# GpSimd's sum of tokens and attention's result in eight pieces, one behind each scatter of sorted rows

## The chip, the cores and the metric

One core of one Trainium2 chip runs the whole program. The metric is the device time of one execution in microseconds; the kernel before took 1020.18 us in the median of 3 runs (1018.56 to 1020.27). TensorE does the matrix products (PE in the rows), VectorE (DVE), ScalarE (ACT) and GpSimd (POOL) the rest, SyncE (SP) issues most transfers. GpSimd issues the scatters, whose addresses are computed in the kernel.

## The reference, cut to what matters

Two layers over x of 2 batches of 1024 tokens with 128 features. Each layer is attention and then a feed-forward part, with a layer norm behind every part. What the change touches is the second half of layer 0:

```
x = x + mla_attention(rmsnorm(x, norm1_w), ...)          # "attention's result" is added to the tokens
x = x + moe(rmsnorm(x, norm2_w), gate_w, gate_b, W1, b1, W2, b2)
x = layernorm(x)

def moe(x, ...):
    logits = x @ gate_w.T + gate_b
    top = argmax(logits)                                   # one of 4 experts for each token
    h = relu(W1[top] x + b1[top]);  return W2[top] h + b2[top]
```

Layer 0 begins with a retention layer of 8 heads and a layer norm; the latent attention has 16 heads of 8 features; layer 1 is an attention with 16 heads and a product with ternary weights.

## The kernel before, in words

All activations stay on the chip: X holds the tokens as 16 tiles of 128 tokens x 128 features (8 tiles for each of the 2 batches), U holds, while the experts work, the result of the latent attention.

The first stage (retention) loops over the 16 tiles. Everything after it is one stage with an order written out by hand: `order()` makes a list of events, (kind, number), and each engine runs through the same list and does its share of every event. So each engine takes its instructions in a fixed order, and waits for the others by semaphores. The base of the list are units of attention: "S" (scores of a unit, TensorE, then exponentials on ScalarE), "A" (scores once more for their maxima, TensorE, then a reduction on VectorE, 12 units ahead), "V" (product with the values). When the maxima of a block are there, "M" turns them and "split" on GpSimd divides them into three bfloat16 parts and writes them with three transfers to the stacks of queries (lines 1331 to 1341). Between the units lie the events of the experts, placed by `experts_of(b)` for batch b (lines 1044 to 1057):

- "square" and "norm": mean square of the tokens, and hn = normalised tokens, with the number of each token behind its features
- "H", "G", "C": logits, the expert of each token, and the row (slot_i) that each token has when tokens are sorted by expert; VectorE writes slot_i at line 1987
- "sort" (lines 1353 to 1359, GpSimd): eight indirect DMAs, one for each tile of 128 tokens, scatter the rows of hn to `sorted_rows` in HBM. Each adds 16 to the semaphore e_sorted
- "steer" and "bias" (VectorE): tables of which expert a tile of sorted rows belongs to
- "base" (lines 1360 to 1366, GpSimd): U = X + U for the batch's eight tiles in one instruction of 128x1024. The helper link() lets GpSimd wait for the instruction's own end. In batch 0 a small product of a bias follows
- `route(b)` on SyncE's queue: load_steer, then load_sorted (line 1211), which waits for e_sorted to be 16 x 8 and loads the sorted rows in three transfers of 4, 4 and 3 tiles, then the weights of each tile's expert (line 1232)
- "x": TensorE transposes the sorted rows (line 1652) as soon as their load has landed; then "h", "y" for 11 tiles (lines 1667 and 1675), "put" (line 1371, GpSimd), which scatters each tile of results back to the order of the tokens, fetch_rows on SyncE, and "sum" (line 1378), which adds U and the fetched rows to X

In the list the event "split" of block 12 comes behind "base" in batch 0; in batch 1 no event of GpSimd stands between "sort" and "base", and the next "split" comes well behind them.

Of the kernel before, what the change touches and what calls it, by code (L numbers as in the profile page):

```python
# [13 lines left out]
ALU = mybir.AluOpType  # L14
# [5 lines left out]
NT = T // P  # L20
# [171 lines left out]
def build(nc, d, out, phases=5):  # L192
    ctx = ExitStack()
    with ctx:
# [21 lines left out]
        X = A.tile(NTILE, P)  # L216
# [10 lines left out]
        U = A.tile(NTILE, P)  # L227
# [134 lines left out]
        def chain(eng, s):  # L362

            def link(ins):
                counts[s.name] = counts.get(s.name, 0) + 1
                ins.then_inc(s, 1)
                eng.wait_ge(s, counts[s.name])
            return link
# [788 lines left out]
        def attention():  # L1157
# [4 lines left out]
            def _(sp):  # L1162
# [57 lines left out]
                def load_steer(b):  # L1220
                    sp.wait_ge(e_steered, b + 1)
                    _, values = nc.values_load_multi_w_load_instructions(
                        whose_i[0:1, 0, :], (mybir.EngineType.SP,), min_val=0, max_val=(NE - 1) * HID,
                        skip_runtime_bounds_check_because="a count of at most 3 of 3 comparisons, times 512")
                    return values
# [76 lines left out]
            def _(pool):  # L1302
                g_ = nc.gpsimd
                link = chain(pool, pool_step)
                for kind, k in order():
# [9 lines left out]
                    elif kind == "ln3":  # L1315

                        t = slice(QT * k, QT * (k + 1))
# [24 lines left out]
                    elif kind == "norm":  # L1342

                        t = slice(k * NT, (k + 1) * NT)
# [8 lines left out]
                    elif kind == "sort":  # L1353

                        pool.wait_ge(e_placed, k + 1)
                        pool.wait_ge(xs_cleared, 16 * B)
                        for t in range(NT):
                            g_.indirect_dma_start(xs_dram[k], bass.IndirectOffsetOnAxis(slot_i[:, t:t + 1], 0),
                                                  hn[:, t, :], None).then_inc(e_sorted[k], 16)
                    elif kind == "base":  # L1360

                        t = slice(k * NT, (k + 1) * NT)
                        link(g_.tensor_tensor(U[:, t, :], X[:, t, :], U[:, t, :], ALU.add))
                        if k == 0:
                            pool.wait_ge(load4, 48)
                            g_.tensor_scalar(bqs, bqk[:, 0:1], QSCALE, None, ALU.mult).then_inc(bias_scaled, 1)
                    elif kind == "put":

                        b, i = k
# [3 lines left out]
                    elif kind == "sum":  # L1373

                        for c in range(2):
                            t = slice(k * NT + QT * c, k * NT + QT * (c + 1))
# [3 lines left out]
                    elif kind == "root":  # L1380

                        t = slice(k * NT, (k + 1) * NT)
# [7 lines left out]
                    elif kind in ("L", "R") and k < 3:  # L1390

                        t = slice(k * QT, (k + 1) * QT)
# [28 lines left out]
            def _(pe):  # L1421
# [9 lines left out]
                for kind, k in order():  # L1431
# [222 lines left out]
                    elif kind == "h":  # L1654

                        b, i = k
                        if i == 0:
                            pe.wait_ge(e_steered, b + 1)
                            _, steer[b] = nc.values_load_multi_w_load_instructions(
                                whose_i[0:1, 0, :], (mybir.EngineType.PE,), min_val=0, max_val=(NE - 1) * HID,  # L1660
                                skip_runtime_bounds_check_because=why)
# [219 lines left out]
            def _(dve):  # L1881
# [19 lines left out]
                for kind, k in order():  # L1901
# [116 lines left out]
                    elif kind == "y":  # L2018

                        b, i = k  # L2020
                        if i == 0:
                            dve.wait_ge(e_steered, b + 1)
                            _, steer[b] = nc.values_load_multi_w_load_instructions(
                                whose_i[0:1, 1, :], (mybir.EngineType.DVE,), min_val=0, max_val=(NE - 1) * P,
                                skip_runtime_bounds_check_because="a count of at most 3 of 3 comparisons, times 128")
# [123 lines left out]
```

## Time and profile before

| what | value |
|---|---|
| median of 3 runs | 1020.18 us (1018.56 to 1020.27) |
| the profiled execution, its own time | 1024.54 us |
| its span (first to last instruction) | 1022.1 us |
| busy: TensorE, VectorE, ScalarE, GpSimd | 890.6, 762.3, 655.0, 392.0 us |
| sum of "base", line 1363 | 2 instructions, 4.0 us |
| scatters of "sort", line 1358 | 16 instructions, 15.7 us |
| chain that ended last, share of the span | TensorE 50%, VectorE 27%, ScalarE 7%, DMA 4%, GpSimd 3% |

Busy time is the time in which an engine executes something; the chain is followed back from the last instruction, at each step to what released it. The experts of batch 0 lie at 444 to 535 us of the span, those of batch 1 at 632 to 740 us. Times in the rows are microseconds from the start of the span.

### The profile page before, as it was taken

The numbers are of one execution on the slowest core, as the hardware profiler recorded it, in microseconds if no ns is written. First come the engines' busy times: TensorE is split into PE (matmuls) and PEld (weight loads), VectorE is DVE, ScalarE is ACT, GpSimd is POOL, SyncE is SP. The second block draws the span as 40 slices with busy tenths as digits, with TensorE's granted clock in tenths as the row PEclk, the third lists the DMA queues.
The fourth block names the chain that finished last, engine by engine and source line by source line (L and its number), as shares of the span: only waits on it lengthen the run. The fifth ranks groups of instructions, "written<-read, shape, count | busy, mean of one in ns | idle before, by whom it ended". The sixth has DMA issues, their size and how long they took to land.

```text
span 1022.1 us, 22793 instructions
## 1 busy us (share of the span) xinstructions
PE 890.6 (87%) x9065; PEld 445.1 (44%) x9070; DVE 762.3 (75%) x1155; ACT 655.0 (64%) x1285; POOL 392.0 (38%) x607
## 2 busy tenths in 40 slices
PE   5999999998877889988798778879988999999983
PEld 3778677777632343333472322216422222222232
DVE  3667766856487678886458498776889999999954
ACT  2554655655526678774446547765767988898981
POOL 2755757878332552134345111352432111111240
PEclk8999999999899999997799899989999999999997
DMA  8000000200501034111420601032206100000000
GB/s 294 1 1 2 1 1 2 73 2 1 150 1 41 21 128 138 38 43 52 122 74 2 199 21 38 5 92 85 75 2 187 32 20 20 21 20 2 5 23 21
DMA packets 49405, 52.51 MB, mean 51 GB/s; under 512 B 8874, under 2 KB 40618, under 8 KB 49140
## 3 DMA queue, kind: packets, MB, share of 16 engines
q1 hardware_dynamic: 45012, 48.12, 15.5%
q0 software_dynamic: 4288, 2.94, 1.1%
q8 instruction: 72, 1.18, 0.5%
q14 instruction: 33, 0.27, 0.1%
HBM read 32.37 MB, written 19.68 MB: 51 GB/s over the span
## 4 chain that ended last, share of the span: by engine, by line
PE 50%; DVE 27%; ACT 7%; issue 6%; DMA 4%; POOL 3%; SPq 2%; another core or an unknown queue 1%; DVEq 0%; ACTq 0%; POOLq 0%
DVE arena L1930 19%; PE banks L1592 10%; PE banks L1557 7%; PE banks L1477 5%; ACT arena L1750 3%; PE banks L740 3%; PE banks L485 3%; PE banks L495 2%; PE banks L1667 2%; PE banks L1675 2%; PE banks L673 2%; DMA arena<-arena 1%; PE banks L735 1%; PE banks L699 1%; ACT arena L521 1%
## 5 line engine op out<-in xcount | busy, mean ns | idle before, releaser
L1930 DVE TENSOR_REDUCE arena<-banks 128x2 f32<-128x1024 f32 (+1 forms) x384 | 440.9, 1198 | 65.4 <-PE banks L1477 33.0
L1750 ACT ACTIVATE arena<-banks 128x512 f32<-128x512 f32 (+1 forms) x768 | 409.4, 587 | 120.9 <-PE banks L1557 77.7
L1592 PE MATMUL banks<-arena 128*9 128x256 f32 (+1 forms) x3328 | 257.0, 385 | 6.8 <-ACT arena L1763 4.6
L1557 PE MATMUL banks<-arena 61*128 61x512 bf16 (+4 forms) x896 | 167.5, 373 | 33.9 <-ACT arena L1750 23.7
L1477 PE MATMUL banks<-arena 56*128 56x512 bf16 (+3 forms) x896 | 165.2, 371 | 29.1 <-DVE arena L1930 22.1
L1557 PEld LDWEIGHTS banks<-arena 61*128 61x128 bf16 (+1 forms) x896 | 44.7, 93 | 194.5 <-ACT arena L1750 160.8
L1331 POOL CAST arena<-arena 16x128 bf16<-16x128 f32 x32 | 9.0, 282 | 301.0 <-ACT arena L1818 292.3
L1592 PEld LDWEIGHTS banks<-arena 128*9 128x9 f32 x3328 | 51.6, 89 | 133.0 <-issue 86.7
L1477 PEld LDWEIGHTS banks<-arena 56*128 56x128 bf16 x896 | 45.2, 95 | 54.6 <-DVE arena L1930 40.9
L383 POOL TENSOR_TENSOR arena<-arena 128x8 f32<-128x8 f32 (+1 forms) x35 | 51.3, 1466 | 30.2 <-DVE arena L2094 27.8
L1341 POOL DMA_DIRECT2D arena<-arena x96 | 55.2, 579 | 10.7 <-POOL arena L1334 9.2
L521 ACT ACTIVATE arena<-banks,arena 128x128 f32<-128x128 f32 x128 | 46.4, 477 | 0.5 <-PE banks L504 0.5
L1371 POOL DMA_INDIRECT expert_rows<-arena x22 | 21.4, 972 | 54.9 <-DVE arena L2026 54.9
L1927 DVE TENSOR_REDUCE arena<-banks 128x4 f32<-128x1024 f32 (+1 forms) x32 | 30.4, 954 | 16.2 <-PE banks L1487 13.5
L511 ACT ACTIVATE arena<-banks 128x1024 f32<-128x1024 f32 x16 | 16.4, 1022 | 39.9 <-PE banks L740 39.9
L554 DVE TENSOR_TENSOR arena<-banks,arena 128x128 f32<-128x128 f32 x16 | 4.7, 291 | 47.0 <-PE banks L495 47.0
L1746 ACT ACTIVATE arena<-banks 128x512 f32<-128x512 f32 (+1 forms) x64 | 27.9, 490 | 17.2 <-PE banks L1566 16.9
L529 ACT ACTIVATE arena<-banks 128x1024 f32<-128x1024 f32 x16 | 16.4, 1026 | 33.9 <-PE banks L485 32.5
L767 DVE TENSOR_TENSOR arena<-banks,arena 128x1024 f32<-128x1024 f32 x16 | 19.6, 1223 | 24.0 <-PE banks L673 23.9
L485 PE MATMUL banks<-arena 128*128 128x128 f32 x256 | 33.9, 287 | 2.6 <-DVE arena L770 2.6
L673 PE MATMUL banks<-arena 128*128 128x512 f32 x64 | 32.8, 637 | 1.7 <-DMA arena<-c_gk 1.7
L866 POOL TENSOR_TENSOR arena<-arena 128x512 f32<-128x512 f32 x16 | 25.3, 1578 | 22.5 <-DVE arena L770 22.5
(239 smaller groups left out, 1463.5 us busy)
## 6 DMA issues: line engine op xcount, KB each, us to landing
arena<-k_products SPq DMA_DIRECT2D x32, 224.0 KB
arena<-q_products SPq DMA_DIRECT2D x64, 112.0 KB
q_products<-arena SPq DMA_DIRECT2D x16, 384.0 KB, 3.3
k_products<-arena SPq DMA_DIRECT2D x16, 384.0 KB, 3.8
arena<-e_w SPq DMA_DIRECT2D x22, 256.0 KB
arena<-arena POOLq DMA_DIRECT2D x96, 4.0 KB, 1.7
sorted_rows<-c_pads SPq DMA_DIRECT2D x2, 709.5 KB, 8.6
arena<-sorted_rows SPq DMA_DIRECT2D x4, 258.0 KB, 3.1
```

Of the source, the lines that this page charges most:

```text
L383: link(eng.tensor_tensor(y, v, epst[:, 1:2].to_broadcast(list(v.shape)), ALU.pow))
L485: ins = nc.tensor.matmul(bank(s // 4)[:, (s % 4) * P:(s % 4 + 1) * P], wg[:, s * P:(s + 1) * P], XT[:, i, :], start=True, stop=True)
L521: ins = nc.scalar.activation(ga[:, s, :], bank(4 + s // 4)[:, (s % 4) * P:(s % 4 + 1) * P], ACT.Identity, scale=gn[:, 0, s:s + 1], bias=gn ...
L673: ins = nc.tensor.matmul(bank(c), XT[:, n + 1, :], wqk[:, c * 512:(c + 1) * 512], start=True, stop=True)
L740: ins = nc.tensor.matmul(bank(2 + s // 4)[:, (s % 4) * P:(s % 4 + 1) * P], sm[:, s, :], vv[n % 2][:, s, :], start=first, stop=True, skip_g ...
L1341: g_.dma_start(rows, nmp[k % 2][:, i, :]).then_inc(mrow[k % 2], 16)
L1477: ins = nc.tensor.matmul(bank(first + par)[:, at:at + hi - lo], Qs[k_][rows, qc, y, qo:qo + P], Ks[k_][rows, y, lo:hi], start=True, stop=n ...
L1557: ins = nc.tensor.matmul(bank(S_BANK + (use + par) % SCORES)[:, at:at + C - o], Ks[n % NS][rows, y, kt * P:(kt + 1) * P], Qs[n % NS][rows, ...
L1592: ins = nc.tensor.matmul(PS[h * VROWS:h * VROWS + VW, AV_BANK, o:end], V[:, b, kt, HG * g + h, :], Pr[u % PROBS][:, h, o:end], start=(kt = ...
L1750: s_.activation(Pr[s % PROBS][:, 2 * x + par, o:C], scores[:, o:C], ACT.Exp) \
L1927: v_.tensor_reduce(of, two_banks.rearrange("p r (y e) -> p r y e", y=2)[:, :, :, 0:width], AX.X, ALU.max).then_inc(ring_dve, 1)
L1930: v_.tensor_reduce(of[:, :, x], two_banks[:, :, 0:width], AX.X, ALU.max).then_inc(ring_dve, 1)
```

## The change

The event "base" no longer does the sum. Each tile's sum now stands directly behind the scatter of that tile in the event "sort", as an instruction of 128x128, and each is linked: GpSimd waits for its end before it takes the next scatter. The bias product of batch 0 stays in "base". What is computed is the same.

```diff
@@ -1355,12 +1355,12 @@
                         pool.wait_ge(e_placed, k + 1)
                         pool.wait_ge(xs_cleared, 16 * B)
                         for t in range(NT):
+                            i = k * NT + t
                             g_.indirect_dma_start(xs_dram[k], bass.IndirectOffsetOnAxis(slot_i[:, t:t + 1], 0),
                                                   hn[:, t, :], None).then_inc(e_sorted[k], 16)
+                            link(g_.tensor_tensor(U[:, i, :], X[:, i, :], U[:, i, :], ALU.add))
                     elif kind == "base":
 
-                        t = slice(k * NT, (k + 1) * NT)
-                        link(g_.tensor_tensor(U[:, t, :], X[:, t, :], U[:, t, :], ALU.add))
                         if k == 0:
                             pool.wait_ge(load4, 48)
                             g_.tensor_scalar(bqs, bqk[:, 0:1], QSCALE, None, ALU.mult).then_inc(bias_scaled, 1)
```

## Rows read from the trace of the kernel before

**Rows 1.** The page: its span, and busy us (share of span) xinstructions.
```profile
span 1022.1 us, 22793 instructions
PE 890.6 (87%) x9065; PEld 445.1 (44%) x9070; DVE 762.3 (75%) x1155; ACT 655.0 (64%) x1285; POOL 392.0 (38%) x607
```
**Rows 2.** Timeline, GpSimd, batch 0: start, duration, engine, line, operation, [idle before <-releaser].
```profile
475.95 1.09 POOL L1358 DMA_INDIRECT sorted_rows<-arena  x1 [7.41 <-DVE arena L1987]
477.35 0.99 POOL L1358 DMA_INDIRECT sorted_rows<-arena  x1 [0.30 <-issue]
...
485.00 0.96 POOL L1358 DMA_INDIRECT sorted_rows<-arena  x1 [0.30 <-issue]
485.99 2.01 POOL L1363 TENSOR_TENSOR arena<-arena 128x1024 f32<-128x1024 f32 x1
...
488.31 0.28 POOL L1331 CAST arena<-arena 16x128 bf16<-16x128 f32 x1
```
**Rows 3.** Timeline, SyncE's queue, batch 0.
```profile
487.29 1.48 SPq L1218 DMA_DIRECT2D arena<-sorted_rows  x3
488.97 25.66 SPq L1232 DMA_DIRECT2D arena<-e_w  x11
```
**Rows 4.** Timeline, TensorE, batch 0.
```profile
488.46 1.04 PE L1592 MATMUL banks<-arena 128*9 128x256 f32 x8
490.29 1.96 PE L1652 MATMUL banks<-arena 128*128 128x128 f32 x8 [0.79 <-DMA arena<-sorted_rows]
```
**Rows 5.** Chain that ended last, batch 0: start, duration, what.
```profile
478.73 8.56 issue
487.29 2.87 DMA arena<-sorted_rows
```
**Rows 6.** Groups by line, GpSimd: shapes, count | busy us, mean ns | idle before, releaser.
```profile
L1332 POOL TENSOR_TENSOR arena<-arena 16x128 f32<-16x128 f32 x32 | 12.9, 402 | 2.7
L571 POOL TENSOR_TENSOR arena<-arena 128x512 f32<-128x512 f32 x6 | 6.5, 1091 | 0.3
L866 POOL TENSOR_TENSOR arena<-arena 128x512 f32<-128x512 f32 x16 | 25.3, 1578 | 22.5 <-DVE arena L770 22.5
L1351 POOL TENSOR_TENSOR arena<-arena 128x1024 f32<-128x1024 f32 x2 | 3.8, 1898 | 0.2
```
**Rows 7.** Timeline, GpSimd, first put of batch 0.
```profile
503.96 1.07 POOL L1371 DMA_INDIRECT expert_rows<-arena  x1 [11.91 <-DVE arena L2026]
```
**Rows 8.** Timeline, GpSimd, batch 1.
```profile
664.92 1.09 POOL L1358 DMA_INDIRECT sorted_rows<-arena  x1 [7.29 <-DVE arena L1987]
...
673.94 0.96 POOL L1358 DMA_INDIRECT sorted_rows<-arena  x1 [0.30 <-issue]
674.93 2.01 POOL L1363 TENSOR_TENSOR arena<-arena 128x1024 f32<-128x1024 f32 x1
685.64 0.28 POOL L1331 CAST arena<-arena 16x128 bf16<-16x128 f32 x1 [8.71 <-issue]
```
**Rows 9.** Timeline, SyncE's queue, batch 1.
```profile
676.32 1.48 SPq L1218 DMA_DIRECT2D arena<-sorted_rows  x3
681.65 31.71 SPq L1232 DMA_DIRECT2D arena<-e_w  x11
```
**Rows 10.** Timeline, TensorE, batch 1, during the scatters.
```profile
670.33 0.62 PE L1592 MATMUL banks<-arena 128*9 128x256 f32 x8
```
**Rows 11.** Transfers issued from 660 to 700 us: KB each, median us to landing.
```profile
arena<-sorted_rows SPq DMA_DIRECT2D x2, 258.0 KB, 3.3
```
**Rows 12.** Timeline, TensorE, batch 1, transposition of sorted rows.
```profile
688.15 0.66 PE L1652 MATMUL banks<-arena 128*128 128x128 f32 x4
```
**Rows 13.** Timeline, ScalarE, batch 0, behind the scatters.
```profile
486.84 2.38 ACT L1750 ACTIVATE arena<-banks 128x512 f32<-128x512 f32 x4 [3.59 <-remote]
```
**Rows 14.** Chain that ended last, batch 1, during the scatters.
```profile
670.07 3.49 another core or an unknown queue
674.67 1.88 another core or an unknown queue
```

## The prediction

> **What bounds the kernel now.** I read the page first, then the timeline of the one engine that the change edits, GpSimd, then the rows of those who wait for it, and last the chain of work that ended last in the same stretch. The page [rows 1] shows TensorE at 87% and GpSimd at 38% of a span of 1022.1 us, so GpSimd is not short of time: 607 instructions and 392 us of work. What it does can only matter where somebody waits for a result of it. The sum X+U of line 1363 is a result that nobody waits for: one instruction of 2.01 us in each batch [rows 2, 8], and nobody needs U before the event "sum", when the experts' rows have been fetched back. The scatters of line 1358 are the opposite.
>
> The rows of GpSimd for batch 0 [rows 2] show eight scatters. The first starts at 475.95 as soon as VectorE has placed the rows (7.41 us idle before it, ended by line 1987). The second starts at 477.35, 0.30 us after the end of the first; the eighth starts at 485.00 and ends at 485.96. So a step of the burst is 0.96 + 0.30 = 1.26 to 1.27 us, and the burst takes 10.01 us. The sum starts 0.03 us behind the last scatter (485.99), and then comes the splitting of the next maxima (488.31).
>
> SyncE waits for all eight scatters together (line 1212: e_sorted at 16 x 8) and issues the loads of the sorted rows at 487.29 [rows 3], 2.29 us after the eighth scatter began (487.29 - 485.00). TensorE has ended its last product before that at 488.46 + 1.04 = 489.50, and its transposition of the sorted rows starts at 490.29 behind 0.79 us of idle time which the load ended [rows 4]. The chain says the same [rows 5]: it goes through a stretch of 8.56 us called "issue", which is SyncE waiting while GpSimd scatters, and then through 2.87 us of the load. So in batch 0 the end of the last scatter sets when TensorE goes on, and TensorE takes its instructions in a fixed order: everything behind the transposition, of all engines, is put off with it. That is the row that decides this case.
>
> **The change, part by part.** Removed: per batch one sum of 128x1024 behind the eight scatters. Added: per batch eight sums of 128x128, one behind each scatter, each with a link(), that is a wait of GpSimd for its own sum before it goes on. Behind that wait stand the next scatter and, behind the last one, the splitting of maxima. Nothing else moves: no DMA is added, and steering, loads and puts keep their places.
>
> The price of a sum of 128x128. The trace has 128x512 at 1.091 us (line 571) and 128x1024 at 1.898 and 2.008 us (lines 1351 and 1363) [rows 2, 6]; from 1.091 to 2.008 is 0.917 us for 512 columns, 0.00179 a column, so 128 columns cost 1.091 - 384 x 0.00179 = 0.40 us. The sum of 16x128 of line 1332, with the same number of columns on fewer partitions, takes 0.402. I take 0.40. Between the end of a scatter and the start of a sum lie 0.03 us [rows 2].
>
> The price of what the sum does to the scatter behind it. There is a gap of 0.30 us ahead of a scatter, whether a scatter stands before it [rows 2] or not; I take it unchanged, with the link's wait inside it. A scatter that follows another kind of instruction took 1.09 us (475.95) and 1.09 us (664.92), and the first put behind other work 1.07 us (503.96), against 0.96 to 0.99 us for one that follows a scatter [rows 2, 7, 8]. In the changed kernel each of the eight follows another kind of instruction. I take 1.07 us; the bounds are 0.97 and 1.09.
>
> So a step becomes 0.03 + 0.40 + 0.30 + 1.07 = 1.80 us instead of 1.27. From the start of the first scatter to the end of the eighth it is 1.09 + 7 x 1.80 = 13.7 us instead of 10.0: **the eighth scatter ends 3.7 us later**. Lower bound: scatters stay at 0.97, step 1.70, 1.09 + 11.9 = 13.0, 3.0 us later. Upper bound: a sum that follows a scatter pays for the change of kind as well, as 2.008 against 1.898 us of the same sum behind other work suggests (0.11 us): step 1.91 to 1.93, 4.5 us later.
>
> Batch 0: the cover of the scatters is gone already (TensorE idles 0.79 us there), so all of it lands on the path: loads issued at 487.29 + 3.7 = 491.0, transposition at 494.0 instead of 490.29. **+3.7 us.** The 2.29 us from the last scatter to the load stay: batch 1 has 676.32 - 673.94 = 2.38 us with the same code [rows 8, 9], and I see nothing in them that a wider spacing shortens. What is late behind it is late by the same amount, because it all hangs from the transposition: the experts' weights are issued behind the sorted loads on the same queue (488.97) [rows 3], and puts, fetch and sum of tokens follow the experts. TensorE's clock: it was already at half speed here (a product group of line 1592 takes 1.04 us at 488.46, against 0.62 us at full clock) [rows 4, 10]. A longer idle stretch might hold it there a little longer; I put zero on it and keep 1.7 us as its upper bound (a further stretch of 3.7 us in which products take 1.04 for 0.62 would lose 3.7 x 0.42/1.04 = 1.5, rounded up).
>
> Splitting of the maxima in batch 0: GpSimd is free after 13.7 + 0.03 + 0.40 = 14.1 us instead of 10.0 + 0.03 + 2.01 = 12.1, that is 2.1 us later. Its three transfers feed scores of block 12, while block 11 has only begun and all of the experts' work stands in between. Zero. Without that cover it would cost up to those 2.1 us.
>
> Batch 1: the eighth scatter ends at 674.90 + 3.7 = 678.6, the loads are issued at 680.0 instead of 676.32 and take 1.48 us to issue, till 681.5. The next thing on SyncE's queue is the first expert weight, which went out at 681.65 [rows 9]: 0.1 us of room, and at the upper bound it goes out 0.7 us late, in front of products at 691.7. The sorted rows land some 3.3 us after issue [rows 11], so at about 683.5 to 685; TensorE transposes at 688.15 [rows 12]. Hidden, and GpSimd itself is idle until 685.64 [rows 8]. **+0.** If the 8.5 us of room were gone it would cost another 3.7.
>
> The removed 2.01 us return nothing: they lie behind the scatters, where nobody waits.
>
> Sum: 0 x 2.01 + 3.7 + 0 = +3.7 us. The profiled execution took 1024.54 us with a span of 1022.1, so 2.4 us lie around the span, and it stands 4.4 us above the median of 1020.18. I expect a span near 1025.8 in a profile, and for the median 1020.18 + 3.7 = **1023.9 us** (+0.36%).
>
> One rule speaks to the price of the sum. In the rows, a sum of 128x512 takes 1.091 us at line 571 and 1.578 us at line 866, a factor 1.45 [rows 6]; the second runs in the first stage, while VectorE is multiplying and adding tiles. The Trainium skill, "GPSIMD Engine Reference", Specifications, says that GpSimd shares its SBUF interfaces with VectorE and contends with VectorE's instructions that have two SBUF inputs. By that rule the small sums, which now run while VectorE makes the steering tables, would be stretched, and the one big sum of before, at 486 us, was not. The trace agrees only in part: VectorE's work beside the burst is mostly reduction out of PSUM.
>
> **The rivals.**
> (a) The sums are stretched by VectorE. Each takes 0.40 x 1.45 = 0.58 us, 7 x 0.18 = 1.3 us more: +5.0 us, 1025.2. For it: 1.578 against 1.091. Against: the scatters themselves kept 0.96 to 0.99 all along, and VectorE's two-input work there is a dozen instructions of 0.2 us.
> (b) Faster: the burst itself disturbs the others, and spreading it mends that. In both bursts ScalarE and VectorE stood still although TensorE's products had been done: ScalarE 3.59 us before 486.84 with an unnamed releaser [rows 13], and in batch 1 the chain has 3.49 and 1.88 us of "unknown queue" [rows 14]. In batch 0 that lies ahead of the wait for the load and is covered by it; in batch 1 it is on the chain. If a step of 1.80 us instead of 1.27 lets it vanish, batch 1 gains 5.4 us and about 2.1 us more, since TensorE's half clock after it vanishes with it (three rounds of scores, maxima and products; where a group of products takes 1.04 for 0.62 us [rows 4, 10], a round loses some 0.7): 3.7 - 5.4 - 2.1 = -3.8 us, 1016.4. It decides from the point where the gain in batch 1 exceeds 3.7 us. Against: it may belong to the profiled execution alone, which is 4.4 us longer than the median, or it goes on for as long as scatters are in flight, and then the longer burst adds some: +1.9 us more, 1025.8.
> (c) No change to measure: half of that disturbance goes (the 3.49 us), 3.7 - 3.5 = +0.2 us, 1020.4; or, with the same outcome, the wait at the transposition has cover in an undisturbed run that I can't see.
> (d) That the change doesn't do what it says: the link's wait might let the next scatter start while the sum runs. The rows speak against it: behind every linked instruction the next one starts only after its end.
>
> **How the numbers follow.** Forecast of +3.7 with its bounds 3.0 to 4.5: 0.62. (a) 0.07. The longer disturbance of (b), 1025.8: 0.05. (b) itself 0.10. (c) 0.14. (d) 0.02: the scatters are then put off by nothing, 1020. A measurement of this kernel can tell about 0.2%, 2.0 us, from no change: slower is all from 1022.2 up, so 0.62 + 0.07 + 0.05 = 0.74; the same 0.14 + 0.02 = 0.16; faster 0.10. The range leaves out (b) and the far end of the late cases: 1020.0 to 1026.0, which takes in (c), the bounds of the forecast, (a), and most of the 1.7 us of the clock.
>
> **What would show it.** In the changed profile: eight sums of 128x128 at 0.39 to 0.58 us between the scatters; scatters 1.70 to 1.93 us apart; SyncE's loads of the sorted rows about 3.7 us later against the first scatter (15.0 instead of 11.3 us behind it) in both batches; TensorE's idle time at line 1652 in batch 0 grown from 0.79 to some 4.5 us, and none in batch 1. It would be wrong if TensorE's wait in batch 0 didn't grow by that, if the unnamed waits of ScalarE vanished or doubled, or if the scatters stayed 1.27 us apart.

## The result, and the profile after

The changed kernel takes 1023.68 us in the median (1022.27 to 1028.81, 8 runs), the kernel before beside it 1020.2 us (1018.56 to 1022.02, 8 runs). The ratio is 1.0049, with a 95% interval of 1.0031 to 1.0067: slower by some 5.0 us (0.0049 x 1020.2) by the ratio, by 3.5 us by the two medians. The profiled executions stand the other way: 1022.82 us with a span of 1020.8 after, 1024.54 us and 1022.1 before [rows 1]. This contradiction is taken up behind the experiments.

The page of the changed kernel, as in rows 1 its span, and busy us (share of span) xinstructions:

```profile
span 1020.8 us, 22812 instructions
PE 886.5 (87%) x9070; PEld 442.6 (43%) x9070; DVE 763.8 (75%) x1155; ACT 654.7 (64%) x1285; POOL 393.8 (39%) x621
```

GpSimd's timeline in batch 0 of the changed kernel, to be read against rows 2 (start, duration, engine, line, operation, [idle before <-releaser]):

```profile
474.18 1.09 POOL L1359 DMA_INDIRECT sorted_rows<-arena  x1 [7.37 <-DVE arena L1987]
475.29 0.43 POOL L1361 TENSOR_TENSOR arena<-arena 128x128 f32<-128x128 f32 x1
476.00 1.00 POOL L1359 DMA_INDIRECT sorted_rows<-arena  x1 [0.28 <-POOL arena L1361]
477.03 0.41 POOL L1361 TENSOR_TENSOR arena<-arena 128x128 f32<-128x128 f32 x1
...
486.22 0.97 POOL L1359 DMA_INDIRECT sorted_rows<-arena  x1 [0.28 <-POOL arena L1361]
487.23 0.42 POOL L1361 TENSOR_TENSOR arena<-arena 128x128 f32<-128x128 f32 x1
...
487.96 0.28 POOL L1331 CAST arena<-arena 16x128 bf16<-16x128 f32 x1
```

The idle time ahead of a scatter is now ended by line 1361, the sum: the link holds the next scatter back. A step is 0.97 + 0.03 + 0.42 + 0.28 = 1.70 us (the first three are 1.82, 1.73 and 1.72) where it was 1.27, and the burst, from the start of the first scatter to the end of the eighth, takes 487.19 - 474.18 = 13.01 us for 10.01.

SyncE's queue in the same kernel, batch 0 and batch 1 (rows 3 and 9 answer to them):

```profile
488.53 1.89 SPq L1218 DMA_DIRECT2D arena<-sorted_rows  x3
490.63 26.15 SPq L1232 DMA_DIRECT2D arena<-e_w  x11
...
681.34 2.92 SPq L1218 DMA_DIRECT2D arena<-sorted_rows  x3
684.53 27.65 SPq L1232 DMA_DIRECT2D arena<-e_w  x11
```

TensorE's timeline, batch 0, and last its transposition in batch 1 (rows 4 and 12):

```profile
484.97 0.62 PE L1592 MATMUL banks<-arena 128*9 128x256 f32 x8
491.45 1.09 PE L1652 MATMUL banks<-arena 128*128 128x128 f32 x4 [5.86 <-DMA arena<-sorted_rows]
493.46 1.09 PE L1652 MATMUL banks<-arena 128*128 128x128 f32 x4 [0.92 <-DMA arena<-sorted_rows]
495.44 1.04 PE L1592 MATMUL banks<-arena 128*9 128x256 f32 x8
...
686.96 0.66 PE L1652 MATMUL banks<-arena 128*128 128x128 f32 x4
```

The wait for the sorted rows in batch 0 was 0.79 us [rows 4] and is 5.86 + 0.92 us. In batch 1 there is none: the loads go out 681.34 - 666.97 = 14.37 us behind the first scatter, before 11.40 [rows 8, 9], and TensorE still comes later than they land.

The chain that ended last, batch 0 of the changed kernel (start, duration, what), runs through the burst and the load, as it did in rows 5:

```profile
474.18 1.09 POOL sorted_rows L1359
475.29 0.44 POOL arena L1361
475.73 0.27 issue
476.00 1.00 POOL sorted_rows L1359
...
486.22 2.29 DMA sorted_rows<-arena
...
488.96 4.36 DMA arena<-sorted_rows
```

Each sum of 128x128 and each 0.27 us behind it is now a piece of the chain. What the profile of after doesn't have is the unnamed waits of rows 13 and 14: during the scatters of batch 1 the chain goes through VectorE and TensorE with no "unknown queue" at all.

The spans are made of stretches that can be compared one by one. From the start of the last put to the end all kernels need 293 to 295 us. The start of the first scatter (474 to 479 us) and the stretch from the last put of batch 0 to the first scatter of batch 1 (135 to 139 us) differ by some microseconds from one execution to the next, the first of them with the same code ahead of it. What an experiment moves is mostly the two stretches from a batch's first scatter to its first put. These are what the table below gives, "scatter to put" for short, from the rows of lines 1358 and 1371 of each profiled execution.

### The profile page after: what moved, and what is told of

It is laid out like the page before. It is cut to its first block, busy times and chain, and to the rows that moved or that the text cites. A ratio compares the mean times of both kernels' runs of the same rounds, so it can differ in the third digit from the quotient of the medians.

```text
span 1020.8 us, 22812 instructions
## 1 busy us (share of the span) xinstructions
PE 886.5 (87%) x9070; PEld 442.6 (43%) x9070; DVE 763.8 (75%) x1155; ACT 654.7 (64%) x1285; POOL 393.8 (39%) x621
## 4 chain that ended last, share of the span: by engine, by line
PE 49%; DVE 28%; ACT 6%; issue 6%; DMA 4%; POOL 4%; SPq 2%; DVEq 0%; ACTq 0%; POOLq 0%
DVE arena L1930 20%; PE banks L1592 10%; PE banks L1557 7%; PE banks L1477 5%; ACT arena L1750 3%; PE banks L740 3%; PE banks L485 3%; PE banks L495 2%; PE banks L1667 2%; PE banks L1675 2%; PE banks L673 2%; DMA arena<-arena 1%; PE banks L735 1%; ACT arena L521 1%; PE banks L699 1%
## 5 line engine op out<-in xcount | busy, mean ns | idle before, releaser
L1927 DVE TENSOR_REDUCE arena<-banks 128x4 f32<-128x1024 f32 (+1 forms) x32 | 30.4, 954 | 14.6 <-PE banks L1487 13.5
```

Of the source, the lines that this page charges most:

```text
L1927: v_.tensor_reduce(of, two_banks.rearrange("p r (y e) -> p r y e", y=2)[:, :, :, 0:width], AX.X, ALU.max).then_inc(ring_dve, 1)
```

## The experiments

Differences are against the kernel before, which ran beside every group of experiments: 1024.37 us in the median beside the first four (1019.43 to 1027.84), 1021.73 beside the next four and 1023.55 beside the last four, which ran on another chip (pieces in one batch "the same again", the change later by one more, and the pause alone). That its own median moves by 4 us between groups, while within a group it serves as the measure, will matter.

| kernel | scatter to put, batch 0 | batch 1 | median us | ratio, 95% |
|---|---|---|---|---|
| before | 28.01 | 31.71 | 1020.2 | |
| the change | 32.02 | 28.50 | 1023.68 | 1.0049 (1.0031 to 1.0067) |
| pieces in batch 0 alone | 31.07 | 31.61 | 1027.56 | 1.0026 (1.0007 to 1.0045) |
| the same again | 30.84 | 31.92 | 1027.37 | 1.0034 (1.0012 to 1.0056) |
| pieces in batch 1 alone | 27.48 | 28.45 | 1020.19 | 0.9967 (0.9949 to 0.9985) |
| the same again | 26.47 | 28.46 | 1020.38 | 0.9962 (0.9941 to 0.9984) |
| eight pieces behind the scatters | 26.65 | 32.40 | 1022.78 | 0.9990 (0.9973 to 1.0007) |
| a second instruction per piece | 35.65 | 31.45 | 1033.07 | 1.0080 (1.0058 to 1.0101) |
| the change again | 29.86 | 27.53 | 1027.43 | 1.0059 (1.0039 to 1.0079) |
| four pieces, batch 1 alone | 27.98 | 29.03 | 1021.95 | 1.0006 (0.9995 to 1.0017) |
| before, experts later | 25.88 | 26.93 | 1016.31 | 0.9945 (0.9926 to 0.9964) |
| the change, experts later | 29.41 | 27.77 | 1020.49 | 0.9992 (0.9976 to 1.0008) |
| the change, later by one more | 28.34 | 27.73 | 1018.52 | 0.9947 (0.9924 to 0.9970) |
| a pause alone, batch 1 | 26.79 | 27.66 | 1019.5 | 0.9957 (0.9935 to 0.9978) |

**One batch at a time.** The sum stays in one piece in the other batch.

```diff
                         for t in range(NT):
+                            i = k * NT + t
...
+                            if k == 0:
+                                link(g_.tensor_tensor(U[:, i, :], X[:, i, :], U[:, i, :], ALU.add))
...
                     elif kind == "base":
-                        t = slice(k * NT, (k + 1) * NT)
-                        link(g_.tensor_tensor(U[:, t, :], X[:, t, :], U[:, t, :], ALU.add))
+                        if k == 1:
+                            t = slice(k * NT, (k + 1) * NT)
+                            link(g_.tensor_tensor(U[:, t, :], X[:, t, :], U[:, t, :], ALU.add))
```

> The eight pieces stand behind the scatters in batch 0 only; batch 1 keeps the one sum of 128x1024. My theory (the whole cost is TensorE's wait for the sorted rows of batch 0): as slow as the full change, +3.0 to +4.0 us, ratio 1.0035 (1.003 to 1.005). Rival (both batches pay, or GpSimd's longer occupation costs by itself): about half of the change, +1.8 us, ratio 1.0018. The eighth scatter of batch 0 should end 13.0 us behind the start of the first, as in the changed kernel, that of batch 1 10.0 us.

With `k == 1` and `k == 0` exchanged:

> The eight pieces stand behind the scatters in batch 1 only; batch 0 keeps the one sum of 128x1024. My theory: batch 1 has 8.5 us of room between the landing of the first sorted rows and their transposition, so no change, within 1 us, ratio 1.000 (0.999 to 1.001). Rival (both batches pay): +1.8 us, ratio 1.0018. Rival of the late signals (the dense burst delays TensorE's signals, and wider spacing mends that in batch 1, where it lies on the chain): up to -5 us, ratio 0.995 to 0.998, and no unnamed wait of ScalarE in batch 1 of the profile, while batch 0 may show one.

Pieces in batch 0 alone cost 0.26%, 2.7 us, and in batch 1 alone they gain 0.33%, 3.4 us. Both were run a second time beside the last group:

> Pieces in batch 0 only, once more. The burst lasts 13.0 instead of 10.0 us, and from its start to the first put it takes 31 us instead of 27.5: +3.5 us, ratio 1.0035 (1.0025 to 1.0045). Rival (parts don't add up, batch 0 bears all of the change's 5 to 6 us): 1.005 or more.

> Pieces in batch 1 only, once more. Two effects are known from traces by now: late signals of TensorE behind a dense burst (31.6 to 32.4 us from the first scatter to the first put of batch 1 where they are, 26.9 where they are not; 27.5 to 28.5 with pieces), and VectorE's tables stretched by the pieces (+0.9 us in batch 1). If the late signals belong to the ordinary runs too: faster again, ratio 0.996 to 0.998. If the first 0.9967 was chance and only the stretched tables are left: ratio 1.000 to 1.002.

The answers were +0.34% (3.5 us) and -0.38% (3.9 us). So the two halves of one change have opposite signs. The batch that loses is the one in which TensorE waits for the sorted rows. The batch that gains is one in which the forecast had seen nothing at all in the sum, and something in its rival (b). Here is ScalarE in batch 1 where the burst is dense (pieces in batch 0 alone, the second time), and VectorE beside it:

```profile
674.17 1.29 ACT L1754 ACTIVATE arena<-banks 128x512 f32<-128x512 f32 x2 [3.50 <-remote]
...
675.59 1.23 DVE L1934 TENSOR_REDUCE arena<-banks 128x2 f32<-128x1024 f32 x1 [2.55 <-remote]
```

and its chain through the same stretch:

```profile
670.66 3.48 another core or an unknown queue
...
675.46 1.67 another core or an unknown queue
```

"Remote" and "unknown queue" mean that the profile finds no releaser. Both engines wait for TensorE's products here, and these had been done for some microseconds (the last section has the rows of one such wait side by side), so by these rows it is TensorE's signal that comes late. The signal itself is in no row, and that both engines waited for something else is not excluded. These are rows 13 and 14 again, in another kernel. Over all 14 profiled executions the picture is: such waits in 9 of the 12 bursts with scatters 1.27 us apart, and in none of the 16 bursts that have something between the scatters. In the rows of batch 1 they are worth 3.8 us: scatter to put takes 31.91 in the mean of the four kernels that have them there (31.71, 31.61, 31.92, 32.40), and 28.07 in the six with eight pieces (28.50, 28.45, 28.46, 27.53, 27.77, 27.73).

**Is it the pieces or their place?** The eight linked sums are kept, but all of them stand behind the eighth scatter.

```diff
                         for t in range(NT):
...
+                        for i in range(k * NT, (k + 1) * NT):
+                            link(g_.tensor_tensor(U[:, i, :], X[:, i, :], U[:, i, :], ALU.add))
                     elif kind == "base":
-                        t = slice(k * NT, (k + 1) * NT)
-                        link(g_.tensor_tensor(U[:, t, :], X[:, t, :], U[:, t, :], ALU.add))
```

> The sum is done in eight linked pieces as in the change, but all of them behind the eighth scatter. My theory (not the pieces cost, but that they stand between the scatters): no change, within 1 us, ratio 1.000 (0.999 to 1.001), though GpSimd works 8 x 0.49 = 3.9 us there instead of 2.0 and the splitting of maxima in batch 0 starts 1.9 us later. Rival (the splitting of maxima or the longer work of GpSimd is what costs): +1.5 to +2 us, ratio 1.0015 to 1.002.

No difference (0.9990, the interval takes in 1), although GpSimd works longer at it:

```profile
486.00 3.87 POOL L1361 TENSOR_TENSOR arena<-arena 128x128 f32<-128x128 f32 x8
```

3.87 us for 2.01, and the splitting of the maxima 1.9 us later, cost nothing. So neither the number of instructions nor GpSimd's time is the price; only what stands ahead of the eighth scatter counts. It also keeps the late signals in both batches, which the pieces between scatters remove.

**Is the dose right?** Each piece gets a second linked instruction, a multiplication of the same 128x128 by 1.

```diff
                             link(g_.tensor_tensor(U[:, i, :], X[:, i, :], U[:, i, :], ALU.add))
+                            link(g_.tensor_scalar(U[:, i, :], U[:, i, :], 1.0, None, ALU.mult))
```

> The change with a second linked instruction of 128x128 behind each piece, a multiplication of U by 1.0 (about 0.3 to 0.4 us with its gap). My theory (every microsecond between the scatters of batch 0 goes 1:1 to the end): 7 x 0.35 = 2.5 us more than the change, about +6.1 us against the kernel before, ratio 1.006 (1.005 to 1.007); still nothing from batch 1. Rival (the delay saturates, or some other wait takes it over): no more than +4.5 us, ratio 1.0045.

GpSimd and TensorE in batch 0 of this kernel:

```profile
481.81 1.06 POOL L1359 DMA_INDIRECT sorted_rows<-arena  x1 [0.28 <-POOL arena L1362]
482.89 0.43 POOL L1361 TENSOR_TENSOR arena<-arena 128x128 f32<-128x128 f32 x1
483.41 0.53 POOL L1362 TENSOR_SCALAR arena<-arena 128x128 f32<-128x128 f32 x1
...
501.59 1.94 PE L1653 MATMUL banks<-arena 128*128 128x128 f32 x8 [10.89 <-DMA arena<-sorted_rows]
```

The burst takes 17.76 us instead of 13.0, and scatter to put in batch 0 35.65 instead of 30.95 (the mean of the four kernels with pieces there and the experts' place unchanged: 32.02, 31.07, 30.84, 29.86): 4.7 us of burst, 4.7 us of path. Batch 1 has run out of room too (31.45 for 28.07). Against the kernel before that is 35.65 - 27.23 = +8.4 in batch 0 and 31.45 - 31.91 = -0.5 in batch 1, +7.9 in all; timed, it is 0.80% of 1024.37, 8.2 us. The forecast of 6.1 us was too low because its dose was: the second instruction lengthens a step by 0.67 us, not by 0.35. In batch 1 TensorE now waits for the sorted rows too, 3.26 us.

**The change once more**, beside the second group:

> The changed kernel itself once more, on the same chip as the next three. With batch 0 alone at 1.0026 and batch 1 alone at 0.9967, three readings are possible. If the parts add up (batch 0 pays about 3.7 us, batch 1 gains about 3.4): 0 to +1 us, ratio 1.000 (0.998 to 1.002). If the first measurement of the change holds: +3.5 to +5 us, ratio 1.0035 to 1.005. In the profile, no unnamed wait of ScalarE or VectorE in either batch.

1.0059: the loss is confirmed, here at 6.0 us (0.0059 x 1021.73), above the range of the second reading, and the parts do not add up to it. The 14 executions of the changed kernel fall into two groups with nothing between them: seven take 1022.3 to 1024.2 us (five of the first eight, two of these six) and seven 1026.7 to 1028.8. Their mean granted clock is 0.959 and 0.956. That the median is 1023.68 the first time and 1027.43 the second is a matter of how many fell into which. Both profiled executions, 1022.82 and 1022.43 us, are of the lower group, so no trace shows what the upper one has.

**How little is enough to keep the gain of batch 1?** Batch 0 stays as before; in batch 1 a sum of two tiles stands behind every second scatter.

```diff
+                            if k == 1 and t % 2:
+                                link(g_.tensor_tensor(U[:, i - 1:i + 1, :], X[:, i - 1:i + 1, :], U[:, i - 1:i + 1, :], ALU.add))
```

> Batch 0 as in the kernel before; in batch 1 the sum is done in four pieces of 128x256, one behind every second scatter, so scatters come in pairs and the mean step is 1.27 + 0.5 x 0.7 = about 1.6 us. If the density of the whole burst delays TensorE's signals (eight scatters in 10 us), the late signals of batch 1 shrink or vanish and the kernel is about 3 us faster than before, ratio 0.997, like the pieces behind every scatter of batch 1. If each scatter has to have its own pause, half or more of the late signals stay (2 to 5 us of unnamed waits in batch 1), ratio 0.998 to 1.000.

The profile shows the burst at 11.99 us, no late signals, and 29.03 us to the put. The time is that of the kernel before (1.0006, up to 1.0017). That is neither of the two expected outcomes: the late signals are gone from the profile and the time is no better. Two things may lie behind it. Beside this group the kernel before had 1021.73 us, so there may have been little to gain. And the longer sums (128x256, 0.65 us) hold up VectorE's tables more: the last of them starts 7.34 us behind the first scatter, against 6.23 in the kernel before and 6.79 in the changed one. The run doesn't settle how wide a pause must be.

**Is it cover that batch 0 lacks?** In the hand-written order the experts of batch 0 (its sorted rows and all behind) are put off by two units of attention, so that TensorE has work while GpSimd scatters. First in the kernel before, then in the changed one, then in the changed one with three units.

```diff
-            pace, tile, end = ((4, 12, 17), (2, 15, 24))[b]
+            pace, tile, end = ((4, 14, 19), (2, 15, 24))[b]
```

> The kernel before with the experts of batch 0 two units of attention later in the order (transposition of the sorted rows, products, puts and sum of tokens), sum in one piece. The wait for the sorted rows gets some 4.5 us more of cover. TensorE's wait at the transposition goes from 0.8 us to 0. If the late signals behind the dense burst are a delay of their own, they are now uncovered and the gain is at most 1 to 2 us, ratio 0.998 to 1.000; the unnamed waits of batch 0 stay. If they cost nothing, 3 us faster, ratio 0.997.

> The changed kernel with the same shift by two units in batch 0. TensorE waits 5.9 + 0.9 us for the sorted rows in the change; two units cover 4.5 us. My theory (the change's loss in batch 0 is this wait and nothing else): 4 to 5 us faster than the change itself, TensorE's wait at the transposition down to 1 to 2.5 us, and faster than the kernel before, ratio 0.996 to 0.999. Rival (the pieces cost time elsewhere in batch 0): no faster than the change by over 1 us.

With (4, 15, 20) in the changed kernel:

> The changed kernel with the experts of batch 0 three units of attention later. Two units left TensorE 2.0 + 0.5 us of waiting for the sorted rows. My theory (in batch 0 the loss is that wait alone): with three units the wait is gone and the kernel is some 1.5 to 2.5 us faster than with two, ratio to before 0.995 to 0.998, and it comes within 1 to 2 us of the kernel before with two units (0.9945). Rival (the pieces cost something else of 3 us or more, that no cover takes away): no faster than with two units, 0.999 or more.

TensorE at the transposition of batch 0 in the three kernels, in this order:

```profile
492.42 0.66 PE L1652 MATMUL banks<-arena 128*128 128x128 f32 x4
493.96 0.63 PE L1652 MATMUL banks<-arena 128*128 128x128 f32 x4 [0.88 <-DMA arena<-sorted_rows]
```
```profile
491.62 0.63 PE L1652 MATMUL banks<-arena 128*128 128x128 f32 x4 [2.04 <-DMA arena<-sorted_rows]
492.75 0.63 PE L1652 MATMUL banks<-arena 128*128 128x128 f32 x4 [0.50 <-DMA arena<-sorted_rows]
```
```profile
495.33 0.66 PE L1652 MATMUL banks<-arena 128*128 128x128 f32 x4
496.29 0.63 PE L1652 MATMUL banks<-arena 128*128 128x128 f32 x4 [0.30 <-DMA arena<-sorted_rows]
```

In the changed kernel the wait of 5.86 + 0.92 us shrinks to 2.04 + 0.50 with two units and to 0.30 with three, and its time against the kernel before goes from 1.0059 to 0.9992 and 0.9947. But the shift also helps the kernel before, by 5.6 us, more than the 3 us that were expected at most; it helps the changed one by 6.8 us, where 4 to 5 were expected. At the same place, two units later, the changed kernel is still 0.47% slower, 4.8 us (0.9992 against 0.9945): TensorE waits 2.54 against 0.88 us, and scatter to put is 3.5 us longer (29.41 for 25.88). Both still wait for their rows there, so the longer burst still shows. Whether the loss goes away when both are covered would need the kernel before with three units, which was not run. So these three runs show that TensorE's wait shrinks with cover and that the time falls by at least as much; they don't show that the pieces cost nothing beside it. That the loss hangs on what stands ahead of the eighth scatter of batch 0 rests on the pieces behind the scatters, on batch 0 alone and on the dose. The kernel before with two units, 1016.31 us (1012.95 to 1018.58) beside 1021.73, beats both kernels of this case.

**Is it the sum or the pause?** In the last experiment the sums stay in one piece in both batches, and in batch 1 GpSimd fills a tile of 192 columns that nobody uses (`spare`) behind each scatter.

```diff
+                            if k == 1:
+                                link(g_.memset(spare, 0.0))
```

> The kernel before, with a linked memset of 128x192 of an unused tile (about 0.4 us, no operand read) behind each scatter of batch 1; the sums stay in one piece. It gives batch 1 the pauses of the change without a GpSimd instruction that reads two operands. If sharing the way to SBUF is what stretches VectorE's tables there: line 2000 stays at 0.21 us where the change shows 0.41 to 0.50, line 1995 at 0.17 instead of 0.49. If the pause keeps TensorE's signals in time: no unnamed waits in batch 1. Time: like the pieces in batch 1 or up to 0.9 us faster, ratio 0.996 to 0.999 if late signals count in ordinary runs, 1.000 if not.

Its batch 1, and then ScalarE in its batch 0, where the burst is dense:

```profile
663.74 1.09 POOL L1360 DMA_INDIRECT sorted_rows<-arena  x1 [7.28 <-DVE arena L1991]
664.81 0.29 POOL L1363 MEMSET arena<- 128x192 f32 x1
665.39 1.01 POOL L1360 DMA_INDIRECT sorted_rows<-arena  x1 [0.29 <-POOL arena L1363]
...
486.21 1.09 ACT L1754 ACTIVATE arena<-banks 128x512 f32<-128x512 f32 x2 [4.28 <-remote]
```

0.9957, a gain of 4.4 us, with work that does nothing but take 0.27 to 0.29 us between scatters. The same execution has a late signal in batch 0 and none in batch 1. So what gains in batch 1 is the pause. Whether it is cheaper this way than by the sums can't be told: 27.66 us to the put is less than their mean of 28.07, but lies within their 27.53 to 28.50, and the intervals of the times overlap.

There is a difference on VectorE, though. Batch 1, the tables of the experts, first in the kernel before, then in the changed one, then with the pause alone (there four lines further down):

```profile
667.24 0.17 DVE L1995 TENSOR_SCALAR arena<-arena 128x12 int32<-128x12 f32 x1
...
670.42 0.21 DVE L2000 SCALAR_TENSOR_TENSOR arena<-arena 128x48 f32<-128x48 f32 x1
670.91 0.21 DVE L2000 SCALAR_TENSOR_TENSOR arena<-arena 128x48 f32<-128x48 f32 x1
```
```profile
669.28 0.49 DVE L1995 TENSOR_SCALAR arena<-arena 128x12 int32<-128x12 f32 x1
...
672.54 0.50 DVE L2000 SCALAR_TENSOR_TENSOR arena<-arena 128x48 f32<-128x48 f32 x1
...
673.32 0.41 DVE L2000 SCALAR_TENSOR_TENSOR arena<-arena 128x48 f32<-128x48 f32 x1
```
```profile
666.05 0.32 DVE L1999 TENSOR_SCALAR arena<-arena 128x12 int32<-128x12 f32 x1
...
669.23 0.21 DVE L2004 SCALAR_TENSOR_TENSOR arena<-arena 128x48 f32<-128x48 f32 x1
```

In the kernel with the sums three instructions grow by 0.32, 0.29 and 0.20 us. Part of the first is covered by the instruction behind it: the last of the tables starts 6.79 us behind the first scatter instead of 6.23, so all three together cost 0.56 us. In the kernel with the filling the first grows by 0.15, line 2004 (line 2000 before) not at all, and the last table starts at 6.22 us.

## Why the prediction was right, and where not

**The time.** Forecast was 1023.9 us and 1023.68 was measured. Part of that is luck: the second time the same kernel had 1027.43 us, the burst grew by less than was forecast, and batch 1, which was put at nothing, holds two terms that were left out. What follows takes the terms one by one.

**The step of the burst: right in kind, one term mis-sized.** Forecast 0.03 + 0.40 + 0.30 + 1.07 = 1.80 us, measured 0.03 + 0.42 + 0.28 + 0.97 = 1.70. The term that failed is the scatter behind another kind of instruction: behind a sum it takes 0.97 us, hardly more than behind another scatter. Only the first of the burst takes 1.09, in both kernels. The evidence in rows 2, 7 and 8 had been scatters behind 7 to 12 us of idle time, never one behind a short sum. The burst grew by 3.0 us, my lower bound, not by 3.7.

**"All of it lands on the path of batch 0: +3.7": the number came out, but not by its working.** Scatter to put is 27.23 us in the mean of the six kernels with the sum in one piece and the experts in their place (28.01, 27.48, 26.65, 27.98, 26.47, 26.79), and 30.95 in the four with pieces: +3.7. Of these 3.0 are the burst: the first transposition starts 14.3 to 14.6 us behind the first scatter in the six and 17.3 to 17.6 in the four. The other 0.7 lies between the first transposition and the put: 12.1 to 13.7 us in the six (mean 12.9), 12.5 to 14.8 in the four (mean 13.6). Two things differ there. In the changed kernel TensorE waits 0.92 us more for the second load, which takes 4.36 us in the chain against 2.87 [rows 5]. And TensorE's clock, whose part I had at zero: the two product groups behind the transposition take 1.04 us each, the half clock, where the stretch is 13.7 us (the kernel before, four pieces) and 0.62 us each, the full clock, where it is 12.1 and 12.2 (pieces in batch 1 the second time, the pause alone). It was at the half clock ahead of the wait as well in the changed kernel, in three groups of four (1.04 us from 479.15 on, 0.62 at 484.97), so the wait is not shown to be what lowers it. As the two ranges overlap, the 0.7 is not clear of noise. Alone in batch 0, timed, the pieces cost 2.7 and 3.5 us.

**"TensorE idles 0.79 us there" was read from a disturbed execution.** The wait grew by 5.07 us at its first part (5.86 - 0.79), more than the burst. In the profile of before TensorE itself had come 2.1 us late to this point, held up by ScalarE's wait for a late signal [rows 13], which hid most of the wait for the load. In the changed kernel TensorE ends its last group ahead of the wait at 484.97 + 0.62 = 485.59, 11.41 us behind the first scatter; in the kernel before the rows had come 490.29 - 475.95 = 14.34 us behind it [rows 2, 4]. So an undisturbed execution of before waits 14.34 - 11.41 = 2.9 us, and the change adds 5.86 - 2.9 = 3.0, the growth of the burst. The kernel with four pieces in batch 1 has the dense burst in batch 0 without late signals, and there the wait stands in a row:

```profile
492.20 1.97 PE L1656 MATMUL banks<-arena 128*128 128x128 f32 x8 [3.28 <-DMA arena<-sorted_rows]
```

So 3.3 us by this execution. The argument survived, since any hole at that point makes the burst critical; the size of the hole did not.

**Splitting of maxima and the room of batch 1: right; the issue of the loads was mis-sized.** The splitting of maxima stood 13.78 us behind the first scatter instead of 12.36, 1.4 us later for the forecast 2.1, and the experiment with the pieces behind the scatters put it off by 1.9 us at no cost. In batch 1 the loads took 2.92 us to issue instead of the 1.48 that I had kept, the first weight went out at 684.53, 0.27 us behind them, and TensorE waited for neither. The removed 2.01 us returned nothing, as forecast.

**"Batch 1: +0" failed.** Two terms were not in the forecast. The late signals, 3.8 us where they occur, go away with the pauses; that is the mechanism of rival (b), and experiment and rows bear it out: -3.4, -3.9, and -4.4 us with the pause alone. I had dismissed it as something that "may belong to the profiled execution alone". Against it stand the four pieces, with no late signal in the profile and no gain in time. And the sums stretch VectorE's tables by 0.56 us. The nearest to a bound for a burst without either is the kernel before with later experts, whose profile has no late signal in batch 1: 26.93 us to the put, against 28.07 with pieces. So batch 1 costs 1.1 us by this one execution where before is undisturbed, and gains 3.8 where it is not.

**Rival (a) fell, its cause turned round.** The small sums took 0.41 to 0.45 us beside VectorE, not 0.58; VectorE's instructions took 0.50 for 0.21. The Trainium skill, "SBUF — State Buffer", Who interferes with whom, states that a VectorE instruction with two SBUF inputs contends with a GpSimd instruction that reads SBUF, and not with one that only writes it. From kernel to kernel the trace agrees: line 2000 has two inputs and takes 0.50 and 0.41 us in the changed kernel and 0.21 in the one with the filling. Row by row it agrees in part. GpSimd at that time, in the changed kernel:

```profile
672.23 0.97 POOL L1359 DMA_INDIRECT sorted_rows<-arena  x1 [0.28 <-POOL arena L1361]
673.23 0.42 POOL L1361 TENSOR_TENSOR arena<-arena 128x128 f32<-128x128 f32 x1
```

VectorE's 0.41 us from 673.32 on lie beside a sum, but the 0.50 from 672.54 on lie beside a scatter, and so do the 0.49 of line 1995, which has one input; in the dense burst scatters leave both lines short. What lengthens those two is open.

**Rival (c)** (no measurable change) fell by the interval, and (d) by the releasers in GpSimd's rows.

**Why slower in time and faster in the profile.** The profiled execution of before has late signals in both batches and costs 1024.54 us, that of the change has none. Batch by batch the rows give 28.01 to 32.02 (+4.0) and 31.71 to 28.50 (-3.2), +0.8 together; the first burst of before began 1.8 us later (475.95 for 474.18), and with that noise the changed profile is the shorter one, by 1.3 us. If most ordinary runs of before had no late signals in batch 1, the change should cost 3.7 + 1.1 = 4.8 us; timed it was 5.0 and 6.0. If most had them, 3.7 - 3.8 = -0.1. The group of the first comparison had a median of before of 1020.2, that of the second 1021.73, while the single batches ran beside 1024.37 and 1023.55. This fits: the parts were measured beside a slower kernel before than the whole was, and so -3.4 and +2.7 need not add up to +5.0. It is argued, not shown, as the ordinary runs leave no rows and the change was not timed beside a before of 1024 us. A second reason is certain: the profiled execution of before, 1024.54 us, is longer than all its eight runs beside the change (1022.02 at most), while the two profiled executions of the change come from the lower of its two groups.

**What stays open.** How often late signals occur in runs without a profile, and what makes them. What makes half of the changed kernel's executions some 5 us longer than the rest. So the 5.0 and 6.0 us of the whole change are not accounted for by its two halves, which together give -0.7 and -0.4. Why the later experts gained 5.6 us in the kernel before, where the rows explain some 3.4: 1.35 to the first put (27.23 to 25.88) and 2.0 from the first put to the last (20.97 for 22.9). Their mean granted clock is higher, 0.963 for 0.959; among the runs of the kernel before beside them 0.001 less goes with 0.43 us more, so the 0.004 would be 1.7 us, an estimate. And the later experts with a pause in batch 1, which together may be better than either, were not tried.

## What to carry to other kernels

Before work is put between the instructions of a burst, find who waits for the last of them: here 3.0 us more of burst became 2.7 and 3.5 us of the kernel in the batch where TensorE had nothing else to do, and TensorE didn't wait for it in the one where it had. Look for cover first: moving the consumer by two units of other work was worth more (5.6 us) than anything done to the pieces. And a profile is one execution: where its own time stands 4 us above the median, an idle time with no named releaser may be all of that difference, and a wait read beside it may be too short. Look at the single times too: where they fall into two groups, ask from which of them the profile comes.

## What the runs showed of the hardware

In 9 of 12 profiled bursts of dense scatters by GpSimd (eight of 128 rows, 1.27 us apart) ScalarE and VectorE stood idle for up to 4.8 us although TensorE's products had been done, with no releaser in the profile. The timelines of TensorE, VectorE and ScalarE in batch 0 of the kernel with the pause in batch 1 alone show it side by side (ScalarE's row is the last one of the fence shown there, 486.21):

```profile
482.14 0.61 PE L1561 MATMUL banks<-arena 59*128 59x512 bf16 x2
482.54 0.63 PE L1481 MATMUL banks<-arena 56*128 56x512 bf16 x2
483.10 1.04 PE L1596 MATMUL banks<-arena 128*9 128x256 f32 x8
486.86 0.60 PE L1561 MATMUL banks<-arena 59*128 59x512 bf16 x2 [2.72 <-ACT arena L1754]
...
486.23 1.23 DVE L1934 TENSOR_REDUCE arena<-banks 128x2 f32<-128x1024 f32 x1 [3.13 <-remote]
```

The scores had been done at 482.14 + 0.61 = 482.75 and ScalarE took them at 486.21; the products for the maxima were done at 483.17 and VectorE took them at 486.23. TensorE then waits for ScalarE in turn, 2.72 us. With anything of 0.27 us or more between the scatters (steps of some 1.5 us and up) none was seen in 15 bursts, nor in the one burst with a pause behind every second scatter. Why a burst has this effect no run shows.

A scatter behind another scatter or a short instruction takes 0.95 to 1.02 us, up to 1.07 with two instructions between; the first of a burst takes 1.09 or 1.10. With sums of 128x128 between the scatters some small VectorE instructions take 0.49 for 0.17 and 0.50 for 0.21 us, and the sums keep 0.41 to 0.45; with a filling, the one with one input takes 0.32 for 0.17 and that of line 2000 keeps 0.21.
